# The written order of five engines is drawn anew in an attention and transformer kernel on one core

## The reference

```python
x = layernorm(x + causal_attention(x))            # 8 sequences x 1024 rows x 256, one head of 64
x = layernorm(x + ffn(x))
# ffn: two layers of
h = shift_token(x); q, k, v = split(h @ wqkv)     # 8 heads of 64
q, k = rotary(l2norm(q) * qs), rotary(l2norm(k) * ks)
x = x + local_attention(q, k, v) @ wo             # windows of 128: own window and the one before
h = layernorm(shift_token(x)) * g + b
a, g = split(h @ w1 + b1); x = x + (a * gelu(g)) @ w2 + b2
```

## Time and profile before

| | us |
|---|---|
| runs | 2681.89, 2685.4, 2693.12; median 2685.4 |
| profiled execution, span | 2682.5 |
| PE busy in the span | 2626.4 |
| DVE, ACT, POOL busy | 2276.5, 1934.8, 1658.1 |

### The profile page before, as it was taken

One profiled execution on the slowest core, in us unless ns is written; L12 is line 12 of the kernel. 1 busy time (PEld: TensorE's weight loads), 2 busy tenths in 40 slices (PEclk: granted clock), 3 DMA queues, 4 the chain that ended last, 5 costly groups with the idle time before them and its releaser, 6 DMA issues.

```text
span 2682.5 us, 65519 instructions
## 1 busy us (share of the span) xinstructions
PE 2626.4 (98%) x22240; PEld 2309.2 (86%) x22240; DVE 2276.5 (85%) x6866; ACT 1934.8 (72%) x4826; POOL 1658.1 (62%) x1753
## 2 busy tenths in 40 slices
PE   8999999999999999999999999999999999999998
PEld 5677688899998899998999898989988999988887
DVE  5778988888888888888888889898989989998786
ACT  5655588777777777777777777777777777778775
POOL 6523755566566556666665676666766667766563
PEclk9999999999999999999999999999999999999999
DMA  9931300000001100000001211011101111111110
GB/s 314 334 105 59 107 21 24 29 24 29 27 27 55 44 25 29 25 29 24 28 25 60 93 31 36 30 37 33 37 30 34 33 33 37 31 36 34 30 32 23
DMA packets 144510, 140.37 MB, mean 52 GB/s; under 512 B 16024, under 2 KB 126128, under 8 KB 143408
## 3 DMA queue, kind: packets, MB, share of 16 engines
q1 hardware_dynamic: 144176, 136.18, 16.0%
HBM read 80.02 MB, written 51.92 MB: 49 GB/s over the span
## 4 chain that ended last, share of the span: by engine, by line
PE 61%; DVE 2%; ACT 1%; issue 1%; DMA 1%; SPq 0%; POOL 0%; DVEq 0%; ACTq 0%; POOLq 0%
PE p_pair L173 13%; PE p_pair L174 10%; PE p_pair L175 10%; PE p_values L2551 6%; PE p_turn L2540 5%; PE p_mixed L173 4%; PE p_mixed L175 4%; PE p_mixed L174 4%; PE p_turn L2522 2%; PE p_turn L2516 1%; PE p_mixed L2486 1%; PE p_mixed L2568 1%; PE p_mixed L2594 0%; PE p_mixed L2593 0%; ACT prob L1224 0%
## 5 line engine op out<-in xcount | busy, mean ns | idle before, releaser
L960 POOL TENSOR_TENSOR prob<-prob,rinv 128x512 f32<-128x512 f32 (+1 forms) x512 | 506.5, 1001 | 393.0 <-DVE rinv L1771 392.7
L1224 ACT ACTIVATE prob<-prob,least 128x256 f32<-128x256 f32 (+1 forms) x1024 | 496.2, 487 | 63.2 <-DVE least L1763 61.7
L938 POOL TENSOR_TENSOR inv_norm<-norm_clipped,minus_half 128x8 f32<-128x8 f32 x256 | 423.0, 1659 | 79.2 <-DVE norm_clipped L1727 71.8
L1763 DVE CUSTOM_DVE_ANT_0 prob<-p_pair,mask,inv_norm 128x256 f32<-128x256 f32 (+1 forms) x1024 | 440.2, 460 | 35.0 <-PE p_pair L175 33.0
L173 PE MATMUL p_pair<-hT_h,w_h 128*128 128x256 f32 (+1 forms) x1408 | 410.1, 291 | 6.9 <-ACT v L1218 2.5
L174 PE MATMUL p_pair<-hT_l,w_h 128*128 128x256 f32 (+1 forms) x1408 | 391.1, 278 | 0.0
L175 PE MATMUL p_pair<-hT_h,w_l 128*128 128x256 f32 (+1 forms) x1408 | 391.0, 278 | 0.0
L1236 ACT ACTIVATE pT<-p_turn 128x512 f32<-128x512 f32 (+1 forms) x512 | 283.7, 569 | 76.3 <-PE p_turn L2540 63.9
L173 PEld LDWEIGHTS p_pair<-hT_h,w_h 128*128 128x128 f32 (+1 forms) x1408 | 262.6, 186 | 22.7 <-issue 10.8
L1835 DVE SCALAR_TENSOR_TENSOR gated<-p_pair,columns,gelu 128x256 f32<-128x256 f32 (+1 forms) x384 | 184.0, 481 | 108.5 <-ACT gelu L1263 106.4
L2540 PE MATMUL p_turn<-ident,prob 128*128 128x128 f32 x1920 | 266.5, 273 | 0.8 <-POOL prob L960 0.5
(11 more groups left out here) (147 smaller groups left out, 7970.3 us busy)
## 6 DMA issues: line engine op xcount, KB each, us to landing
x_tile<-x_rows SPq DMA_DIRECT2D x192, 128.0 KB, 2.1
a_wraw<-in_w_all SPq DMA_DIRECT2D x32, 264.0 KB, 5.3
w_high<-a_wraw_h SPq DMA_DIRECT2D x32, 264.0 KB, 3.9
w_low<-a_wraw_l SPq DMA_DIRECT2D x32, 264.0 KB, 4.7
a_x<-in_x SPq DMA_DIRECT2D x32, 256.0 KB, 4.2
x_rows<-a_x SPq DMA_DIRECT2D x64, 128.0 KB, 1.8
x_tile<-x_rows SPq DMA_DIRECT2D x128, 64.0 KB, 2.0
mid_rows<-x_mid SPq DMA_DIRECT2D x128, 64.0 KB, 1.7
```

The costliest lines, as they stand in the source:

```text
L938: pool.tensor_tensor(r[:, t.slot(2), heads], rt[:, heads], half[:, heads], ALU.pow).then_inc(pool_r[n], 1)
L960: pool.tensor_tensor(p, p, rinv[:, 2 * m:2 * m + 2].unsqueeze(2).to_broadcast([P, 2, cols.stop - cols.start]), ALU.mult).then_inc(pool_p, 1)
L1224: act.activation(prob[:, h, cols], prob[:, h, cols], ACT.Exp, bias=least[:, h:h + 1], scale=-1.0, accum_out=rsum[:, h:h + 1]).then_inc(act ...
L1763: dve.tensor_tensor_reduce(prob[:, h, cols], p_score[h % 2][:, c0 + cols.start:c0 + cols.stop], mask[:, a.slot(2), cols], r[:, a.slot(2), ...
```

## The change

All five streams are written in another order. The operations, their operands, buffers and semaphores stay. The repeated part covers steps 12 to 59 on PE, ACT and DVE (before: from 11 on PE, 9 on ACT and DVE) and 11 to 59 on SP and POOL (before: from 8). The steps before that are written out in `first_on_...`. The core of the diff, one period of PE:

```diff
-            turn_probs(T(6), 3)
             project_v(T(4))
-            turn_probs(T(5), 0)
             turn_x(T(3))
-            scores(T(5), 1)
+            turn_probs(T(6), 3)
             values(T(6), 0)
...
             values(T(6), 3)
-            project_k(T(3), 0)
-            project_k(T(3), 1)
-            turn_h(Q(4))
-            turn_q(T(4))
-            turn_probs(T(5), 1)
+            scores(T(5), 1)
             project_q(T(3))
+            turn_probs(T(5), 0)
+            turn_probs(T(5), 1)
+            turn_h(Q(4))
+            project_k(T(3), 0)
+            project_k(T(3), 1)
+            turn_q(T(4))
             turn_k(T(4))
             output(T(6))
             project_v(T(3))
             turn_probs(T(5), 2)
             turn_probs(T(5), 3)
             scores(T(4), 0)
             values(T(5), 0)
...
             values(T(5), 3)
+            after((dve_least, T(4), H, 4))
+            scores(T(4), 1)
             widen(Q(4), 0)
+            after((act_v, T(3), 1, 1))
             widen(Q(4), 1)
-            scores(T(4), 1)
-            turn_k(T(3))
-            output(T(5))
+            after((dve_gt, Q(4), HF + 1, 1))
             widen(Q(4), 2)
             widen(Q(4), 3)
             turn_q(T(3))
+            output(T(5))
+            turn_k(T(3))
             widen(Q(4), 4)
             turn_x(T(2))
             widen(Q(4), 5)
-            turn_probs(T(4), 0)
-            turn_probs(T(4), 1)
             scores(T(3), 0)
+            turn_probs(T(4), 0)
+            turn_probs(T(4), 1)
             project_k(T(2), 0)
...
```

DVE, ACT and POOL around those places:

```diff
 # DVE
-            k_low(T(4))
             q_low(T(4))
-            clip(T(4), 0)
-            rope_cos(T(3), 0)
             middle(T(6))
+            clip(T(4), 0)
+            k_low(T(4))
             rope_sin(T(3), 0, 0)
-            h_low(Q(4))
             rope_sin(T(3), 0, 1)
+            h_low(Q(4))
+            q_sum(T(3))
             least_of(T(4), 0)
             least_of(T(4), 1)
             least_of(T(4), 2)
             least_of(T(4), 3)
-            q_sum(T(3))
...
 # ACT
-            v_out(T(3))
             probs_out(T(5), 2)
             probs_out(T(5), 3)
             exponential(T(4), 0)
             exponential(T(4), 1)
             exponential(T(4), 2)
-            o_high(T(5))
             exponential(T(4), 3)
+            v_out(T(3))
+            o_high(T(5))
             gelu(Q(4), 0)
...
 # POOL
             normalise(T(5), 3)
             inverse_norms(T(4), 0)
-            inverse_norms(T(3), 1)
             k_sum(T(3))
+            final_inverse_std(T(10))
+            final_inverse_std(T(9))
+            inverse_norms(T(3), 1)
             k_scaled(T(3))
...
```

More of the change, by code:

```diff
@@ new lines, in first_on_vector @@
+    t.middle(T(12))
+    t.k_low(T(14))
+    t.h_low(Q(10))
+    t.rope_cos(T(15), 0)
+    t.rope_sin(T(15), 0, 0)
+    t.rope_sin(T(15), 0, 1)
+    t.least_of(T(14), 0)
+    t.least_of(T(14), 1)
+    t.least_of(T(14), 2)
+    t.least_of(T(14), 3)
+    t.q_sum(T(15))
+    t.norms(T(15), 1)
+    t.clip(T(15), 1)
+    t.least_of(T(14), 4)
+    t.least_of(T(14), 5)
+    t.least_of(T(14), 6)
+    t.least_of(T(14), 7)
+    t.o_low(T(13))
+    t.clip(T(15), 0)
+    t.gated(Q(10), 0)
+    t.inverse_sums(T(14), 0)
@@ new lines, in first_on_vector @@
+    t.normed(T(12))
+    t.normed(T(13))
+    t.x_low(T(17))
+    t.least_of(T(15), 4)
+    t.least_of(T(15), 5)
+    t.least_of(T(15), 6)
+    t.least_of(T(15), 7)
+    t.clip(T(16), 0)
+    t.q_sum(T(16))
+    t.h_affine(Q(12))
+    t.final(T(7))
+    t.final(T(8))
+    t.o_low(T(14))
+    t.rope_cos(T(17), 1)
+    t.rope_sin(T(17), 1, 0)
+    t.rope_sin(T(17), 1, 1)
+    t.inverse_sums(T(15), 1)
+    t.norms(T(17), 1)
+    t.q_low(T(16))
+    t.k_low(T(16))
+    t.rope_cos(T(17), 0)
+    t.rope_sin(T(17), 0, 0)
@@ new lines, in first_on_vector @@
+    t.final(T(9))
+    t.rope_sin(T(17), 0, 1)
+    t.q_sum(T(17))
+    t.h_low(Q(12))
+    t.least_of(T(16), 0)
+    t.least_of(T(16), 1)
+    t.least_of(T(16), 2)
+    t.least_of(T(16), 3)
+    t.middle(T(14))
+    t.clip(T(17), 1)
+    t.inverse_sums(T(16), 0)
+    t.o_low(T(15))
+    t.least_of(T(16), 4)
+    t.norms(T(17), 0)
+    t.clip(T(17), 0)
+    t.gated(Q(12), 0)
+    t.gated(Q(12), 1)
+    t.gated(Q(12), 2)
+    t.final(T(10))
+    t.final(T(11))
+    t.least_of(T(16), 5)
+    t.q_low(T(17))
@@ new lines, in first_on_vector @@
+    t.q_sum(T(18))
+    t.o_low(T(16))
+    t.h_affine(Q(14))
+    t.rope_cos(T(19), 0)
+    t.final_statistics(T(13))
+    t.inverse_sums(T(17), 1)
+    t.rope_cos(T(19), 1)
+    t.rope_sin(T(19), 1, 0)
+    t.rope_sin(T(19), 1, 1)
+    t.q_low(T(18))
+    t.middle(T(16))
+    t.clip(T(18), 0)
+    t.k_low(T(18))
+    t.rope_sin(T(19), 0, 0)
+    t.rope_sin(T(19), 0, 1)
+    t.h_low(Q(14))
+    t.q_sum(T(19))
+    t.least_of(T(18), 0)
+    t.least_of(T(18), 1)
+    t.least_of(T(18), 2)
+    t.least_of(T(18), 3)
@@ new lines, in first_on_vector @@
+    t.norms(T(19), 0)
+    t.least_of(T(18), 4)
+    t.norms(T(19), 1)
+    t.gated(Q(14), 0)
+    t.clip(T(19), 1)
+    t.final(T(12))
+    t.inverse_sums(T(18), 0)
+    t.final(T(13))
+    t.gated(Q(14), 1)
+    t.o_low(T(17))
+    t.least_of(T(18), 5)
+    t.least_of(T(18), 6)
+    t.least_of(T(18), 7)
+    t.gated(Q(14), 2)
+    t.clip(T(19), 0)
+    t.gated_low(Q(14), 0)
+    t.gated(Q(14), 3)
+    t.middle(T(17))
+    t.gated_low(Q(14), 1)
+    t.gated_low(Q(14), 2)
+    t.q_low(T(19))
+    t.k_low(T(19))
@@ L5955, in first_on_tensor @@
     a.values(7, 2)
+    a.output(7, 1)
+    t.project_v(T(0))
+    a.scores(7, 4)
+    a.values(7, 3)
     t.after((signal.act_v, T(0), 1, 1))
@@ L6414, in first_on_tensor @@
     t.output(T(7))
+    t.after((signal.act_v, T(10), 1, 1))
+    t.project_k(T(10), 0)
+    t.project_k(T(10), 1)
+    t.after((signal.dve_mid, T(7), 1, 1))
+    t.narrow(T(3))
     t.after((signal.act_pT, T(8), 4, 1))
```

5648 lines of the change are left out of this document (2904 added, 2744 removed).

## The result

| | before | after |
|---|---|---|
| runs, us | 2681.89, 2684.4, 2685.4, 2693.12 | 2848.89, 2851.56, 2853.13, 2861.24 |
| median | 2684.9 | 2852.35 |
| ratio after/before | | 1.0626, 95% interval 1.0602 to 1.0649 |
| profiled execution, span | 2682.5 | 2849.8 |

The four runs of before are the three known at the time of the forecast and one more. The forecast was 2740 us, range 2664 to 2766. The direction was right, the size was not: +55 forecast, +167 measured. The kernel after is outside the range.

The account below looks back on a forecast made before the run. PE's instructions, not waits, were taken to bound the middle. Terms without the lock gave +11, the lock +48 - 5 more: +54, rounded to +55 on 2682.5; with 2.9 for the runs' median, 2740 us, range 2664 to 2766.

Parts of the forecast that it names:

- Where the bound lies: Middle, 300 to 2400 us: bound by PE's instructions, not waits; PE idle only 8.9 us.
- Part 1: PE: fewer excursions (going from wide to narrow matmuls and back); -9.6 us over 48 periods, -5 outside the repeated part.
- Part 2: PE's widen(Q, 2) comes too early and waits for gated(Q, 0): 0.4 us per period, +19 us.
- Part 3: Second scores of T(4) waits for least_of, as k_sum on POOL blocks q_sum on DVE: 1.0 us per period, +48.
- B: Rival: DVE wins the tie, so q_sum isn't blocked by k_sum; 2696 us, range 2685 to 2710, chance 0.25.
- C: Rival: producers arrive in time everywhere and only the excursions count; 2666 us, chance 0.22.
- D: Rival: the lock strikes q_sum(T(4)) also, three least_of 1.1 us late; +26 over 24 periods, 2766 us, chance 0.08.
- its own chance of 0.45: Chance of the predicted main case: POOL leads and k_sum blocks q_sum; 2740 us, own range 2715 to 2765.
- Part 4: project_v(T(3)) has less work before it after project_k, so may wait: 0.05 us per period, +2 us.
- Part 5: Moved loads, load_x1, residual_x1, final, final_inverse_std and swaps in the attention block: all costed at nothing.
- Start and end: Tiles before step 12 and last_steps go narrow 25 and 27 times fewer: -9.4 us, taken as -5.

Follow-up runs that it names:

- six moves: The five moves plus, on POOL, residual_x1(T(6)) from ahead of inverse_norms(T(2), 1) to behind k_scaled(T(2)), against the changed kernel: 2702.52 us, 1.0071 to before.
- `v_out` early: Changed kernel with v_out(T(3)) on ACT moved from behind exponential(T(4), 3) to behind k_high(T(4)): 2837.74 us, 1.0565 to before.
- moving `k_sum`: Changed kernel with k_sum(T(3)) on POOL moved behind the two final_inverse_std, which exist in layer 1 alone: 2829.38 us, 1.0536 to before.
- the five moves: Changed kernel with q_sum behind least_of, k_low ahead of two gated_low, normed earlier, both residual later and v_out earlier, together: 2714.8 us, 1.0111 to before.
- `q_sum` behind: Changed kernel with q_sum(T(3)) on DVE moved back behind the four least_of of T(4): 2816.39 us, 1.0483 to before.
- `normed` early: Changed kernel with normed(T(5)) on DVE put ahead of inverse_sums(T(3), 0), in place of normed(T(7)) in the next step: 2833.53 us, 1.0550 to before.
- `residual` late: Kernel with `normed` early, and on POOL residual(T(6)) and residual(T(5)) moved behind inverse_std(T(5)): 2805.49 us, 1.0458 to before.
- the control above: Layer 0 of the kernel that moved k_sum behind the finals, same program there as the changed kernel: 943.6 us against 943.4.
- the last kernel of the table: Kernel before with scores(T(4), 1) on PE moved ahead of widen(Q(4), 0) and (Q(4), 1), directly behind values(T(5), 3): 2685.25 us, 0.9997 to before.

## Why the prediction was wrong, point by point

- **Where the bound lies**: right. The middle had 8.9 us to give, and a new order could only lose there.
- **Part 1, -15 us: wrong.** The one excursion of the repeated step, taken alone, gave -1.4 us (-3.5 to +1.9) for -9.6; six moves, which have all the fewer excursions, reach layer 0 of before and not less. Two steps failed. "Between `scores` and `values` nothing of that kind shows" is false, the gap is there; that a like gap at the way out had been missed as well made the borders come out at 0.15 for 0.2 by luck. And the sum took it without a word that all other matmuls keep their spacing, and `widen`'s did not (0.118 for 0.114). The rule cited there, of the Trainium skill, "TensorEngine Tiling (Array Packing)", section Key Properties, said that this change costs a drain too; the 0.20 us at 1118.47 agrees.
- **Part 2, +19: right in mechanism, a little high.** `v_out` early gives back 15, PE waits 14.5 us for `gated` in 50 waits. But it isn't a term of its own "on top" of part 3: with `q_sum` moved alone 5.8 us of it are left.
- **Part 3, +48: right in mechanism and nearly in size.** 39.2 us of waits, 36 taken back by moving `q_sum`, 0.95 us per period by moving `k_sum`. Rivals B and C are out, and so is D: `q_sum(T(4))` at 1115.54 takes 0.69 us, and at 2033.07 in layer 1 0.68. Its `k_sum` starts only at 1116.75. That POOL came first at `q_sum(T(3))` rests on 0.07 us, which the forecast had as 0.06 from two sums: the side was right, but a good part of that was luck, as its own chance of 0.45 says.
- **Part 4, +2:** `project_v(T(3))` starts 0.06 us later after `output` in layer 0 (1.57 us for 1.51) and not later in layer 1, so about +1.4. With six moves, where fewer waits stand ahead of it, it is 0.10 later in both layers (1.61 and 1.63). No run isolates it.
- **Part 5, 0: this is the step that failed.** The forecast looked for blocks at `q_sum` alone (part 3 and rival D) and had no term for any other DVE call that the new order puts beside POOL's work. The runs showed 40 us for `k_low` behind two blocked `gated_low` and 47 for the two `normed`, and 12 for `residual_x1`: 99 of the 112 us that the forecast missed. `residual_x1` it had named, with `inverse_norms` and `k_scaled` behind it, "which PE needs some 5 us later"; PE came to `turn_k` 0.7 us (17.1/25) before `k_scaled` was done. For `gated_low` I had the row in hand: the earlier trace rows shows one at 1.24 us beside a POOL instruction, and I used it to price `q_sum`. `normed` the forecast's rule left out, for it speaks of instructions that read two tiles in SBUF, and `normed` has one.
- **Start and end:** I had forecast -5 for both. The end (from pair 112 on) takes 273.6 us in both kernels. Of the steps ahead of the repeated part, those from pair 8 to 16 take 160.9 for 146.7, with waits of the same kinds (`gated`, `k_scaled`, `x_low`), but those from pair 0 to 8 take 149.2 for 156.5, so together they lose 7 us and not the 14 on which I built in the expectation of the five moves. Pair 0 itself starts 5 us later, within the scatter given below. In the two profiled executions the 167 us are then 60 in layer 0, 95 in layer 1, 7 from pair 0 to 16 and 5 ahead of pair 0. The 7 us were not tried by themselves.

The rule of the Trainium skill, "SBUF — State Buffer", section Who interferes with whom, names the calls I missed: two-input instructions on SBUF, and `tensor_scalar`, which may enter a mode that takes the same port. The traces agree (`gated_low` 1.26 for 0.43, `normed` 1.71 for 0.60, `clip` 0.99 for 0.16). I had weighed the rule for one pair of instructions where it is a rule for the whole period. In one point the traces differ: beside `inverse_norms`, whose POOL instruction also reads SBUF but only 8 columns, a two-input DVE instruction isn't held up. In after 49 `q_sum` run inside one and take 0.69 us at most, as here, POOL first:

```profile
1115.14 1.64 POOL L958 TENSOR_TENSOR inv_norm<-norm_clipped,minus_half 128x8 f32<-128x8 f32 x1 [1.50 <-DVE norm_clipped L1747]
1115.54 0.69 DVE L1754 TENSOR_TENSOR q_rot<-rope_cos,rope_sin 128x512 f32<-128x512 f32 x1
```

## What to carry to other kernels

When an order is drawn anew, lay POOL's work on whole SBUF tiles beside DVE's for a whole period, and price every DVE instruction with two SBUF tiles, or a TENSOR_SCALAR on SBUF, that comes to stand beside it: each can end some tenths of a microsecond after POOL's does. In a kernel whose producers end just in time, each such block goes straight to PE; where a producer has room, as `q_sum` had in before, it costs nothing. Single cures give the size of the whole (138 us against 137.6) but not its parts: by layer the sum was off by 9 us one way and 17 the other, because a cure frees the next wait. And before a gap is priced by counting one kind of border, look at the last instruction of each group at every kind of border.

## What the runs showed of the hardware

- A blocked DVE instruction doesn't appear as idle: its time is in its length. The sum of a line's busy time over its count shows it (`q_sum` 1.23 against 0.71 us).
- TENSOR_SCALAR with one SBUF tile is blocked too, even at 8 columns (0.99 us for 0.16). TENSOR_REDUCE is not: in before 29 `norms` run wholly inside a `normalise` that started first, and all take 0.68 us, as here:

```profile
590.47 1.04 POOL L960 TENSOR_TENSOR prob<-prob,rinv 128x512 f32<-128x512 f32 x1 [1.67 <-DVE rinv L1771]
590.66 0.68 DVE L1720 TENSOR_REDUCE norms_sq<-squares 128x8 f32<-128x512 f32 x1
```

- A blocked instruction ends a fixed time after the POOL instruction that held it, the same each time to 0.01 us and for every POOL call: 0.55 us for 512 columns of two inputs (`q_sum`, 49 times in after: 1126.12 against 1125.57 above), 0.28 for 256 columns (`gated_low`, 92 times), 0.08 for the TENSOR_SCALAR of 128 columns (`normed`), 0.03 for that of 8 columns (`clip`). For the two-input ones that is 1.07 to 1.09 ns per column, so by an estimate from these numbers nearly all of the instruction's own work comes after the release, and hardly any of it is hidden in the wait.
- A long wait can cost PE twice. In layer 1 of after every fourth period waits over 2 us for `x_low` (2.12 at 2030.6); after that one the granted clock is 0.50 (1.2 of 2.4 GHz) for 3.4 us, and the matmuls of `project_q` start 0.43 us apart for 0.23:

```profile
2029.60:2033.00 3.40, 1.28 (x15) 1.06 (x14) 3.40 (x8) 0.60 (x1) 2.59 (x4) 1.00 0.00 0
2033.00:2036.40 3.40, 3.40 (x12) 2.71 (x12) 2.57 (x10) 1.75 (x7) 3.27 (x3) 0.50 0.00 0
2036.40:2039.80 3.40, 3.40 (x26) 3.08 (x25) 2.12 (x5) 3.07 (x8) 1.92 (x3) 1.00 0.00 0
```

  That is 3.4/2 = 1.7 us each time. Such stretches stand at 1708.7, 2033.0, 2196.8 and 2360.7, behind four of the six long waits (those that end at 1870.7 and 2522.8 have none), 7 us in all; with `q_sum` behind it was three of six. The 23 waits of 1.0 to 1.24 us in layer 1 with `normed` early had none behind them. What decides between two long waits no run shows. With `normed` early and `residual` late the long waits are gone from layer 1, and so are the stretches: part of the 33.7 us that the two moves gave back there.
- The first 340 us vary by themselves: `h_low` of pair 0 starts at 333.4 to 348.2 us in the ten kernels whose instructions up to there are the same. So a few microseconds between two spans say nothing. The times between two calls inside the repeated part agree to a few tenths (943.4 and 943.6 us in the control above), unless a single long wait falls in one of them, as the 3.7 us of the last kernel of the table.
